# Turning the second layer's outputs with VectorE's 32 by 32 blocks in place of TensorE

## The reference

```python
x = _layernorm(x + L0(x, adj, ...))
x = _layernorm(x + L1(x, adj, ...))   # its last step: out = _batchnorm(h @ W2.T + b2, g2, be2)
x = _layernorm(x + L2(x, adj, ...))   # two graph convolutions, then LSTMs over windows of 1 to 4 nodes
x = _layernorm(x + L3(x, adj, ...))   # eight Euler steps
```

## Time and profile before

| | |
|---|---|
| median of three runs | 922.88 us (922.36 to 925.52) |
| the profiled execution | 921.94 us, of which the span 920.1 us |
| mean granted TensorE clock | 0.994 of full speed |
| PE busy | 886.2 us, 96% of the span |
| DVE, ACT, POOL busy | 72%, 61%, 37% |
| one steady step of a group | 83.7 us |

### The profile page before, as it was taken

The page is one execution under the profiler, slowest core; times in us unless marked ns, Lnnn a source line. Parts: engine busy times, 40 slices in busy tenths (PEclk is TensorE's granted clock), DMA queues, the critical chain, the costliest instruction groups (busy, mean ns, idle before and its releaser), DMA issues.

```text
span 920.1 us, 14508 instructions
## 1 busy us (share of the span) xinstructions
PE 886.2 (96%) x4970; PEld 768.7 (84%) x4970; DVE 663.5 (72%) x1574; ACT 565.0 (61%) x1234; POOL 340.5 (37%) x548
## 2 busy tenths in 40 slices
PE   9999998988989999999999999999999999999996
PEld 6888985466877799888989898898989899978986
DVE  6988886876687866677677667767676777665744
ACT  6576756934755774677378547745763775466341
POOL 3768775630122520352153136214421631340221
PEclk9999999999999999999999999999999999999999
DMA  5422201320110101012001201010120001001000
GB/s 188 150 69 69 69 24 66 141 69 1 34 59 0 35 12 47 1 47 62 8 13 35 70 1 36 24 58 1 47 69 1 12 12 47 1 11 36 1 24 23
DMA packets 26594, 38.54 MB, mean 42 GB/s; under 512 B 3333, under 2 KB 12422, under 8 KB 26010
## 3 DMA queue, kind: packets, MB, share of 16 engines
q1 hardware_dynamic: 26088, 36.05, 11.8%
q10 hardware_dynamic: 434, 1.57, 0.5%
HBM read 21.89 MB, written 15.73 MB: 41 GB/s over the span
## 4 chain that ended last, share of the span: by engine, by line
PE 52%; DVE 11%; ACT 6%; POOL 6%; issue 4%; ACTq 0%; DVEq 0%; POOLq 0%
PE psum L141 15%; PE psum L143 14%; PE psum L142 14%; PE psum L1860 2%; PE psum L1864 2%; PE psum L1861 2%; ACT gate L1433 1%; POOL out_rstd L1366 1%; POOL node_l L1384 1%; DVE x L1634 1%; DVE x_stats L1612 1%; DVE in_h L1602 1%; POOL x_rstd L1366 1%; ACT raw L1464 1%; PE psum L1900 1%
## 5 line engine op out<-in xcount | busy, mean ns | idle before, releaser
L1433 ACT ACTIVATE gate<-psum,gate_bias 128x256 f32<-128x256 f32 (+2 forms) x296 | 143.7, 556 | 61.6 <-PE psum L1864 50.9
L141 PE MATMUL psum<-in_h,wih_h 128*128 128x256 f32 (+2 forms) x312 | 107.6, 345 | 7.5 <-DVE in_l L1606 5.0
L143 PE MATMUL psum<-in_h,wih_l 128*128 128x256 f32 (+2 forms) x312 | 104.1, 334 | 0.0
L142 PE MATMUL psum<-in_l,wih_h 128*128 128x256 f32 (+2 forms) x312 | 103.6, 332 | 0.0
L1400 POOL TENSOR_TENSOR gate<-in_h,in_l 128x512 f32<-128x512 f32 x14 | 17.9, 1306 | 157.5 <-DVE in_l L1606 157.5
L141 PEld LDWEIGHTS psum<-in_h,wih_h 128*128 128x128 f32 x312 | 59.2, 190 | 19.4 <-DVE in_l L1606 9.0
L1436 ACT ACTIVATE gate<-cell 128x512 f32<-128x512 f32 (+2 forms) x80 | 40.3, 503 | 50.7 <-DVE cell L1590 39.9
L1587 DVE TENSOR_TENSOR gate<-gate 128x256 f32<-128x256 f32 (+2 forms) x48 | 24.2, 504 | 59.4 <-ACT gate L1433 59.3
L142 PEld LDWEIGHTS psum<-in_l,wih_h 128*128 128x128 f32 x312 | 59.5, 191 | 5.5 <-issue 0.5
L143 PEld LDWEIGHTS psum<-in_h,wih_l 128*128 128x128 f32 x312 | 59.3, 190 | 4.8
L141 PE MATMUL psum<-e_h,shared 128*128 128x384 f32 x180 | 61.4, 341 | 0.2
(11 more groups left out here) (395 smaller groups left out, 2887.4 us busy)
## 6 DMA issues: line engine op xcount, KB each, us to landing
x_spill<-x SPq DMA_DIRECT2D x30, 256.0 KB, 2.0
xt<-in_x_t_dram SPq DMA_DIRECT2D x16, 256.0 KB, 2.8
raw<-x_spill SPq DMA_DIRECT2D x16, 256.0 KB, 2.9
o_spill<-xt SPq DMA_DIRECT2D x14, 256.0 KB, 2.0
xt<-o_spill SPq DMA_DIRECT2D x14, 256.0 KB, 3.4
x<-x_spill SPq DMA_DIRECT2D x14, 256.0 KB, 3.5
out_dram<-raw SPq DMA_DIRECT2D x14, 256.0 KB, 2.3
raw<-in_adj_t_dram ACTq DMA_DIRECT2D x1, 1024.0 KB, 8.8
```

What stands on the lines that cost most here:

```text
L141: pe.matmul(dst, lh, rh, start=start, stop=False, **kw)
L142: pe.matmul(dst, lh, rl, start=False, stop=False, **kw)
L143: return pe.matmul(dst, ll, rh, start=False, stop=stop, **kw)
L1433: nc.scalar.activation(gate[q][:, 0:n], banks[GATE_BANK[q]][:, 0:n], ACT.Tanh if q == 2 else ACT.Sigmoid, bias=gate_bias[:, p - 1, q:q + 1 ...
```

## The change

The 14 batches that come from DRAM are turned in two other stages, and PE has no part in it.

- **Fetch.** A 128 by 128 tile is 4 by 4 blocks of 32 by 32. SP fetches o2 in four DMAs (one for each 32 partitions), each block at the place that it has in the transposed tile, not turned in itself. A run of 32 numbers (128 bytes) is contiguous on either side, and a batch has 2048 of them, where it had 128 rows of 2048 bytes.
- **Scale and shift.** Now a partition holds four features, one for each column block, so ACT `prep` is four instructions over 128 by (4 by 32) with columns of a new tensor `norm2_blocks`. At the start of the second half, a DVE copy (`selectors`, 128 by 512) and four small matmuls (`block_columns`) spread scale and shift over it, and a DVE copy takes it out of PSUM.
- **Turn.** DVE turns the 32 by 32 blocks with one instruction, from `o2[j]` to `pre[:, j, :]`, in its own `turn`, ahead of the add, which now reads `pre` and not PSUM. It waits for ACT's `prep`, and the add waits for it.
- PE's `turn` is gone from all lists but START; its waits for the PSUM bank are now in `gather0`.

```diff
-        FILL_PE = [[], ["giant_2", "giant_3", "giant_0", "giant_1", "turn_0"], ["x3t_0", "power1a_0"],
-                   ["power1b_0", "power2_0", "gather0_0"], ["coefs0_0", "weight0_0"], ["coefs1_0", "turn_1"],
+        FILL_PE = [[], ["giant_2", "giant_3", "giant_0", "giant_1"], ["x3t_0", "power1a_0"],
+                   ["power1b_0", "power2_0", "gather0_0"], ["coefs0_0", "weight0_0"], ["coefs1_0"],
...
-                sp.dma_start(o2[j], o2_dram[b]).then_inc(front_loaded[j], 16)
+                by_node = o2_dram[b].rearrange("(a i) (t q k) -> q i t a k", a=blocks, q=blocks, k=side)
+                for q in range(blocks):
+                    rows = o2[j][side * q:side * (q + 1), :].rearrange("i (t a k) -> i t a k", a=blocks, k=side)
+                    sp.dma_start(rows, by_node[q]).then_inc(front_loaded[j], 16)
...
-                if not at_start(n):
-                    act.wait_ge(front_loaded[j], 32 * g)
-                elif n == 0:
+                if n == 0:
                     return
-                nc.scalar.activation(o2[j], o2[j], ACT.Identity, scale=scale2[:, 0:1], bias=shift2[:, 0:1]).then_inc(normed2, 1)
+                if at_start(n):
+                    ins = nc.scalar.activation(o2[j], o2[j], ACT.Identity, scale=norm2[:, 0:1], bias=norm2[:, 1:2])
+                else:
+                    act.wait_ge(front_loaded[j], 16 * (blocks + 1) * g)
+                    act.wait_ge(columns_kept, 1)
+                    for a in range(blocks):
+                        part = o2[j].rearrange("p (t a k) -> p a t k", a=blocks, k=side)[:, a, :, :]
+                        ins = nc.scalar.activation(part, part, ACT.Identity, scale=norm2_blocks[:, a, 0:1], bias=norm2_blocks[:, a, 1:2])
+                ins.then_inc(normed2, 1)
...
-                dve.wait_ge(o2_turned, n + 1)
-                nc.vector.tensor_tensor(flat(x2[j]), FB[j][:], flat(x2[j]), ALU.add).then_inc(x2_summed, 1)
+                if at_start(n):
+                    dve.wait_ge(o2_turned, n + 1)
+                    nc.vector.tensor_tensor(flat(x2[j]), FB[j][:], flat(x2[j]), ALU.add).then_inc(x2_summed, 1)
+                else:
+                    dve.wait_ge(normed2, n)
+                    dve.wait_ge(h_ready, n - GB + 1)
+                    nc.vector.transpose(pre[:, j, :], o2[j]).then_inc(o2_turned, 1)
+                    dve.wait_ge(o2_turned, n + 1)
+                    nc.vector.tensor_tensor(flat(x2[j]), pre[:, j, :], flat(x2[j]), ALU.add).then_inc(x2_summed, 1)
...
+            def block_columns():
+                pe.wait_ge(lws_ready, 2)
+                for a in range(blocks):
+                    mm = pe.matmul(banks[0][:, P + 2 * a:P + 2 * (a + 1)], bp[:, 5 + a, :], norm2[:], start=True, stop=True)
+                mm.then_inc(weff_done, 1)
```

More of the change, by code:

```diff
@@ L70, in program @@
         ident = whole.enter_context(nc.sbuf_tensor("ident", [P, P], F32))
[L71 to L72 removed]
+        norm2 = whole.enter_context(nc.sbuf_tensor("norm2", [P, 2], F32))
+        scale2, shift2 = norm2[:, 0:1], norm2[:, 1:2]
         adj_h, adj_l = sb("adj_h", [P, NT, N], F32R), sb("adj_l", [P, NT, N], F32R)
@@ L963, in second_half @@
         x2 = [x1_pair[:, (B - 1 - j) % 2, :, :] for j in range(GB)]
+        blocks = 4
+        side = P // blocks
+        norm2_blocks = sb("norm2_blocks", [P, blocks, 2])
         node_h, node_l = sb("node_h", [P, NT, D], F32R), sb("node_l", [P, NT, D], F32R)
@@ L1221, in second_half @@
         TAIL_SP = [["out_0", "out_1"], ["outhalf_1", "outhalf_0"]]
-        START_PE = ["turn_0", "turn_1", "weff", "first_0", "first_1", "gather0_0", "gather0_1", "weight0_0", "weight0_1", "first_2",
+        START_PE = ["turn_0", "turn_1", "weff", "first_0", "first_1", "block_columns", "gather0_0", "gather0_1", "weight0_0", "weight0_1", "first_2",
                     "gather1_0", "gather1_1", "weight1_0", "weight1_1"]
@@ L1226, in second_half @@
                      "first_2", "gather1_0", "gather1_1", "input_0", "input_1"]
-        START_DVE = ["columns", "turn_0", "turn_1", "weff", "conv_bias", "first_0", "row_sum", "first_1", "gather0_0", "gather0_1", "weight0_0", "weight0_1",
+        START_DVE = ["columns", "turn_0", "turn_1", "weff", "conv_bias", "selectors", "first_0", "row_sum", "first_1", "block_columns", "gather0_0", "gather0_1", "weight0_0", "weight0_1",
                      "first_2", "bcols", "gather1_0", "gather1_1", "weight1_0", "input_0", "weight1_1", "input_1"]
@@ L1230, in second_half @@
         START_SP = ["norm_0", "norm_1"]
-        ONCE_PE = [[], ["turn_0", "first_3", "square"], ["cube", "second_0"], ["gather0_0", "fourth", "second_1"],
-                   ["weight0_0", "fc_0"], ["turn_1", "fc_1"], ["gather1_0", "fc_2", "second_2"], ["weight1_0"],
+        ONCE_PE = [[], ["first_3", "square"], ["cube", "second_0"], ["gather0_0", "fourth", "second_1"],
+                   ["weight0_0", "fc_0"], ["fc_1"], ["gather1_0", "fc_2", "second_2"], ["weight1_0"],
                    ["gather0_1"], ["weight0_1", "second_3"], ["gather1_1", "offset", "weight1_1"]]
@@ L1243, in second_half @@
         ONCE_SP = [["prep_0", "prep_1"], [], ["norm_0"], [], ["ahead_0"], [], ["norm_1"], [], [], [], ["x3load"]]
-        NEXT_PE = [["hlate"], ["lift", "turn_0", "bias"], ["x3t_0", "power1a_0"], ["power1b_0", "power2_0", "gather0_0"],
-                   ["weight0_0", "coefs0_0"], ["coefs1_0", "turn_1"]] + FILL_PE[6:]
+        NEXT_PE = [["hlate"], ["lift", "bias"], ["x3t_0", "power1a_0"], ["power1b_0", "power2_0", "gather0_0"],
+                   ["weight0_0", "coefs0_0"], ["coefs1_0"]] + FILL_PE[6:]
         NEXT_ACT = [[], ["lift"] + FILL_ACT[1], FILL_ACT[2] + ["split_e"], ["power1_0", "power2_0", "evens_l", "gather0_0"],
@@ L1830, in _ @@
                             "x3t": x3t, "innersum": inner_sum, "innerlow": inner_low, "ysum": ysum, "outsum": outsum,
-                            "columns": columns, "conv_bias": conv_bias_rows, "row_sum": row_sum, "weff": weff, "bcols": spread_bias, "square": square, "cube": cube,
+                            "columns": columns, "conv_bias": conv_bias_rows, "row_sum": row_sum, "weff": weff, "selectors": selectors, "block_columns": block_columns, "bcols": spread_bias, "square": square, "cube": cube,
                             "fourth": fourth, "fc": fc, "mix": mix, "offset": offset, "bias": bias, "first": lambda t: low(0, t), "second": lambda t: low(1, t),
@@ L1882, in gather @@
                     pe.wait_ge(x2_lo, n + 1)
+                    if not at_start(n):
+                        pe.wait_ge(pre1_ready, GB * g)
+                        need(pe, x3_summed, GB * (g - 1))
+                        need(pe, pre0_ready, n if j == 1 else 0)
                 else:
@@ L2081, in _ @@
                             "inner": inner, "giant": giant, "hturn": hturn,
-                            "weff": weff, "first": lambda t: product(0, t), "second": lambda t: product(1, t),
+                            "weff": weff, "block_columns": block_columns, "first": lambda t: product(0, t), "second": lambda t: product(1, t),
                             "square": square, "cube": cube, "fourth": fourth, "fc": fc, "offset": offset, "lift": lift, "bias": bias},
```

17 lines of the change are left out of this document (10 added, 7 removed).

## The result

| | before | after |
|---|---|---|
| median | 924.19 us (922.36 to 925.58, 5 runs) | 931.61 us (929.06 to 932.08, 5 runs) |
| the profiled execution | 921.94 us, span 920.1 | 931.75 us, span 930.0 |
| one steady step | 83.70 us | 84.88 us |

The changed kernel is slower by 0.8%: ratio 1.0082, 95% interval 1.0065 to 1.0098. The forecast was 933.4 us, with 925.5 to 940 as its range.

What follows compares the result with a forecast made beforehand. It took the round through DVE, ACT and POOL from `giant` to cell 7 as the bound; 7.2 (steady steps) + 2.1 (step 0) + 1.0 (step 1) + 0.2 (constants) = 10.5 us on 922.88, giving 933.4 us, range 925.5 to 940.

Steps and rivals of the forecast that it cites:

- the round: Stretch from `giant`'s end to cell 7 through DVE, ACT and POOL, 39.9 us; claimed to set pace, adding 1.44 us a step.

Runs made afterwards that it cites:

- one version: Changed kernel with the whole turn (transpose, add, statistics) moved off its place to idle slots: 922.88 us against 922.35 for the kernel before, steady step 82.59 us.
- the fastest version: Changed kernel from group 3 on, groups 1 and 2 left to PE, `turn_0` moved whole, of `turn_1` only the transpose: 916.91 us against 923.31 before, ratio 0.9938.
- the first three experiments: Kernel before plus DVE's transpose, 930.14 us; changed kernel without DVE's transpose, 923.45; kernel before without PE's transposes, 922.23; each against 922.35 for the kernel before.

## What to carry to other kernels

A busy share of 96% doesn't say that an engine sets the pace: look for a wait that repeats in every step, however short, and follow it back, for then work taken off the busy engine buys only a longer wait, and each instruction added to the round costs most of its length (here 0.56 and 0.64 us of 0.74). When a change frees work from a resource (here a PSUM bank), ask where that work can go now: the same transpose cost 1.2 us a step ahead of its add, nothing that shows in an idle place, and with `turn_0` moved off the round altogether the change gained 0.56 over the same move with PE's transposes. And read totals by stage: one version gained 1.1 us in each steady step and lost it all in the first two.

## What the runs showed of the hardware

- **A DVE instruction with two sources in SBUF can be held up by a large one on POOL.** In the fastest version DVE's add takes 1.47 us beside POOL's sum of two parts (five of its ten, those at `turn_0`) and 0.68 elsewhere; the transpose ahead of it, beside the same POOL instruction, keeps its 0.70. DVE, then POOL, same kernel:

```profile
615.10 0.70 DVE L1657 STREAM_TRANSPOSE xt<-xt 128x512 f32<-128x512 f32 x1
615.83 1.47 DVE L1666 TENSOR_TENSOR x<-xt,x 128x512 f32<-128x512 f32 x1
```

```profile
614.20 2.56 POOL L1416 TENSOR_TENSOR gate<-in_h,in_l 128x512 f32<-128x512 f32 x2 [21.21 <-DVE in_l L1629]
```

In every kernel here the same stands on the round itself, where I had not seen it: DVE's `st_l` of cell 5, 340 columns wide, takes 1.59 us beside POOL's `x3split_1` and 0.51 in the cell before. After, DVE and POOL:

```profile
592.16 1.59 DVE L1610 TENSOR_TENSOR st_l<-gate,st_h 128x340 fp32r<-128x340 f32 x1
```

```profile
592.08 1.30 POOL L1400 TENSOR_TENSOR shared<-raw,shared 128x512 fp32r<-128x512 f32 x1 [11.49 <-ACT shared L1516]
```

The Trainium skill has the rule in SBUF — State Buffer, section SBUF: two separate sides: DVE with two SBUF inputs and GpSimd (where it reads SBUF) take one pair of ports in turn, and the loser waits for the whole instruction. The trace agrees in both places: the add ends 0.54 us and `st_l` 0.37 us behind the POOL instruction, and the one-source transpose is not held up. It bears on this change, and the prediction left it out: the changed add has both sources in SBUF, where it had one in PSUM. In the changed kernel no large POOL instruction stood beside it; where the add was moved to slot 10, one did. No run took the POOL instruction away.

- **The clock can fall once and cost 1.5 us, in some executions and not in others.** From one output's store to the next load (`raw<-x_spill`) in the last step but one lie 25.08 us before and 26.65 in the run without PE's transposes, whose clock there is 0.95; the code of that stretch is the same. The 29 executions of before beside the first three experiments say the same: the six with a mean granted clock of 0.992 took 923.64 to 924.56 us, the six with 0.996 took 921.25 to 922.35.

```profile
822.18:847.26 25.08, 23.23 (x140) 21.84 (x140) 14.37 (x36) 17.53 (x44) 2.68 (x3) 1.00 0.05 15
```

```profile
820.46:847.11 26.65, 24.82 (x142) 23.41 (x141) 14.46 (x36) 17.72 (x44) 2.42 (x3) 0.95 0.05 14
```

  A difference of 1 or 2 us between two single executions of this kernel is no evidence; the step times are.
